# A shifted-window layer followed by a Fourier layer: one clamp moves to GpSimd, the second normalisation is written back to PSUM, and the transposes of x move between the halves of the second MLP layer

## The reference, cut to what matters

```
# layer 0, per window of 4x4 positions, 4 heads of 16 channels
qkv = xw @ qkv_w.T + qkv_b
qn = q / max(norm(q), 1e-12);  kn = k / max(norm(k), 1e-12)
attn = softmax(qn @ kn.T * scale + bias)
a = (attn @ v) @ proj_w.T + proj_b
x = x + layernorm(a) * g1 + b1
h = gelu(x @ fc1_w.T + fc1_b) @ fc2_w.T + fc2_b
x = x + layernorm(h) * g2 + b2
# layer 1: moving average over the rows plus a learned filter on the first 128
# Fourier modes of what is left; here it is a product with one matrix per channel
```

## Time and profile before

| what | value |
|---|---|
| median of 3 runs | 7964.86 us (7961.18 to 7968.6) |
| the profiled execution, its own time | 7957.41 us |
| its span on the core | 7955.6 us |
| PE busy | 6613.9 us (83%) |
| DVE busy | 6520.1 us (82%) |
| ACT busy | 5628.4 us (71%) |
| POOL busy | 5096.5 us (64%) |
| granted TensorE clock | 0.979 of full speed |

### The profile page before, as it was taken

One profiled execution on the slowest core, in us unless ns is written; L12 is line 12 of the kernel. 1 busy time (PEld: TensorE's weight loads), 2 busy tenths in 40 slices (PEclk: granted clock), 3 DMA queues, 4 the chain that ended last, 5 costly groups with the idle time before them and its releaser, 6 DMA issues.

```text
span 7955.6 us, 278088 instructions
## 1 busy us (share of the span) xinstructions
PE 6613.9 (83%) x105272; PEld 4133.5 (52%) x105272; DVE 6520.1 (82%) x8543; ACT 5628.4 (71%) x7004; POOL 5096.5 (64%) x4616
## 2 busy tenths in 40 slices
PE   8788888888888888888888888888888887787786
PEld 5544444444444444444444444444444444676675
DVE  1599999999999999999999999999999997222221
ACT  1488888888888888888888888888888888222221
POOL 0477777777777777777777777777777776000000
PEclk9899999999999999999999999999999999898898
DMA  2355555555555555555555555555555554999999
GB/s 98 112 148 147 146 145 145 146 147 146 146 146 146 146 146 146 145 145 146 147 147 146 147 146 146 147 146 146 144 145 147 147 146 124 331 332 354 342 332 338
DMA packets 1486082, 1370.67 MB, mean 172 GB/s; under 512 B 670097, under 2 KB 1080081, under 8 KB 1481875
## 3 DMA queue, kind: packets, MB, share of 16 engines
q1 hardware_dynamic: 1481412, 1235.63, 56.7%
q10 hardware_dynamic: 4608, 134.22, 4.0%
HBM read 412.97 MB, written 285.21 MB: 88 GB/s over the span
## 4 chain that ended last, share of the span: by engine, by line
DVE 49%; issue 29%; PE 14%; DMA 4%; DVEq 2%; ACT 0%; SPq 0%; POOL 0%; ACTq 0%; POOLq 0%
PE ps L632 10%; DVE arena L861 8%; DVE arena L879 8%; DVE ps L918 4%; DVE arena L884 4%; DVE arena L849 4%; DVE arena L933 4%; DVE arena L912 4%; DMA out<-arena 4%; DVE arena L899 4%; DVE arena L927 2%; DVE arena L873 2%; DVE arena L855 2%; PE ps L466 1%; DVEq L230 1%
## 5 line engine op out<-in xcount | busy, mean ns | idle before, releaser
L607 PE MATMUL ps<-mats,arena 128*64 128x512 f32 x4096 | 1083.3, 607 | 506.4 <-ACT mats L730 501.7
L595 PE MATMUL ps<-arena 64*128 64x512 f32 x4096 | 1017.5, 613 | 459.1 <-DVE arena L840 459.0
L997 POOL TENSOR_TENSOR arena<-arena 128x1024 f32<-128x1024 f32 x512 | 980.1, 1914 | 270.2 <-DVE arena L840 270.2
L730 ACT ACTIVATE mats<-ps,arena 128x1024 f32<-128x1024 f32 x1024 | 1133.1, 1107 | 0.0
L1004 POOL TENSOR_TENSOR arena<-arena 128x512 f32<-128x512 f32 x1024 | 1122.2, 1115 | 4.1 <-PE ps L551 4.1
L632 PE MATMUL ps<-rows,mats 128*128 128x256 f32 x4096 | 916.9, 388 | 234.6 <-ACT arena L751 159.4
L1036 POOL TENSOR_TENSOR arena<-arena 128x512 f32<-128x512 f32 x512 | 541.7, 1058 | 742.4 <-DVE arena L893 742.4
L963 DVE COPY arena<-ps 128x512 f32 x256 | 269.3, 1067 | 880.5 <-PE ps L632 564.0
L632 PEld LDWEIGHTS ps<-rows,mats 128*128 128x128 f32 x4096 | 796.9, 195 | 355.0 <-ACT arena L751 163.3
L595 PEld LDWEIGHTS ps<-arena 64*128 64x128 f32 x4096 | 373.5, 185 | 1129.7 <-issue 586.4
L1042 POOL TENSOR_TENSOR arena<-arena 128x512 f32<-128x512 f32 x512 | 566.8, 1107 | 544.7 <-DVE arena L906 544.7
(11 more groups left out here) (94 smaller groups left out, 15274.2 us busy)
## 6 DMA issues: line engine op xcount, KB each, us to landing
arena<-arena SPq DMA_DIRECT2D x1024, 256.0 KB, 2.7
rows<-arena SPq DMA_DIRECT2D x4096, 64.0 KB, 2.0
arena<-in_x SPq DMA_DIRECT2D x1024, 128.0 KB, 2.8
arena<-arena SPq DMA_DIRECT2D x1024, 128.0 KB, 2.3
y<-ystripe SPq DMA_DIRECT2D x512, 256.0 KB, 3.3
mats<-mix SPq DMA_DIRECT2D x512, 256.0 KB, 3.4
rows<-y SPq DMA_DIRECT2D x512, 256.0 KB, 4.1
out<-arena ACTq DMA_DIRECT2D x32, 4096.0 KB, 27.2
```

What stands on the lines that cost most here:

```text
L595: ins = mm(M[:, a, :], w1[a * C:a * C + C, kk * P:(kk + 1) * P], x1T[ring(g, 2)][a * C:a * C + C, :], start=True, stop=True, tile_position ...
L607: ins = mm(H2[a * C:a * C + C, :], w2[:, kk, :], hT[kk][:, a, :], start=(kk == 0), stop=(kk == 1), tile_position=(0, a * C))
L730: f(hT[kk], M, ACT.Gelu, bias=b1[:, kk:kk + 1]).then_inc(done, 1)
L997: tt(sq, q, q, ALU.mult).then_inc(squared, 1)
```

## The change

Three edits. `clamp` (a maximum with 1e-24 of 128 x 64 numbers) is taken from DVE and put on POOL, between `expand_v` and `add2`; `sum_squares` now waits until the clamp of the group before has read its input. `normed2` writes its result back into H2 instead of dn2 (the tile goes away), `gain2` reads H2, and `second_layer` waits for `gain2` (`yg_sb`) instead of `normed2` (`dn2_sb`). On PE, `turn_x` moves from ahead of `project` to between the two halves of `second_layer`.

```diff
-        sq1, sq1x, sq2, dn2, yg = (carve(512) for _ in range(5))
+        sq1, sq1x, sq2, yg = (carve(512) for _ in range(4))
...
                         if kk == 0:
                             need(pe, gelu0, g)
-                            need(pe, dn2_sb, before(g))
+                            need(pe, yg_sb, before(g))
...
                 scores(i4)
-                turn_x(i0)
                 project(i7)
                 second_layer(i9, 0, fc2a_ps)
+                turn_x(i0)
                 second_layer(i9, 1, fc2b_ps)
...
                 def sum_squares(g):
                     if there(g):
                         need(dve, squared, g)
+                        need(dve, clamped, before(g))
...
-                def clamp(g):
-                    if there(g):
-                        need(dve, summed, g)
-                        need(dve, logged, before(g, 2))
-                        ts(ssc[ring(g, 2)], ss, 1e-24, None, ALU.max).then_inc(clamped, 1)
...
-                        stt(dn2, H2, be2, r12[:, 1, :], ALU.add, ALU.mult).then_inc(dn2_sb, 1)
+                        stt(H2, H2, be2, r12[:, 1, :], ALU.add, ALU.mult).then_inc(dn2_sb, 1)
...
-                        ts(yg, dn2, g2, o12, ALU.mult, ALU.add).then_inc(yg_sb, 1)
+                        ts(yg, H2, g2, o12, ALU.mult, ALU.add).then_inc(yg_sb, 1)
...
                 sum_squares(i2)
-                clamp(i2)
                 bias(i4)
...
+                def clamp(g):
+                    if there(g):
+                        need(pool, summed, g)
+                        need(pool, logged, before(g, 2))
+                        settled(pool)
+                        pool.tensor_scalar(ssc[ring(g, 2)], ss, 1e-24, None, ALU.max).then_inc(clamped, 1)
...
                 expand_v(i5)
+                clamp(i2)
                 add2(i10)
```

## The result

The changed kernel takes 7743.22 us (median of 4 runs, 7742.71 to 7744.98) against 7963.02 us before (7959.75 to 7968.6): 0.9724 of the time, 95% interval 0.9707 to 0.9741. It is 220 us faster, where 348 were forecast; the measured time lies inside the stated range of 7480 to 7790 us.

What follows compares the result with a forecast made beforehand. DVE, 96% busy, bounded the 12.57 us step; then a loop through H2 would, at 6.08 + 3.74 + 1.66 + 0.39 = 11.87 us. Saving 0.70 x 502 = 351 us gives 7615 us, range 7480 to 7790.

Steps and rivals of the forecast that it cites:

- DVE was the bound and is not any more: Layer 0: DVE, 96% busy, bounds the old step; afterwards it needs 11.01 us and idles ahead of `normed1`.
- The clamp leaves DVE for almost nothing on POOL: Clamp: takes 1.19 us per step from DVE and costs POOL about 0.3 us, for which POOL has room.
- The rival that ended on the slower side: Clamp on POOL: above 1.83 us it exceeds the old step; at 2.5 us the kernel takes 8301 us; slower, chance 0.05.
- The new wait: PE's second layer waits for `gain2`, closing a one-step loop over PE, ACT and DVE that sets the step at 11.87 us.
- The size of the loop: Loop through H2: ACT 6.08, DVE 3.74, PE 1.66, hand-overs 0.39, together 11.87 us, with ends 11.63 and 12.35.
- The way from the transposes to `log_norms`: Part of the loop through H2, added up over ACT: `keep_x`, table load, `square2`, norms, exponentials; 0.31 us idle left out.
- The dearer loop: Rival at `normed2` and `gain2`: PSUM pause or POOL wait lengthens the loop to about 12.15 us, 7754 us; chance 0.20.
- By itself the transposes' move costs no instruction: PE: moving `turn_x` adds no instruction, starts `project` 0.58 us earlier, but puts 0.66 us of transposes in the loop.
- The fast form never runs at its speed here, so the edit gains: `gain2` on DVE: out of SBUF it waits for POOL, slot 0.97 us; out of PSUM 0.68 us, slot 0.60.

Runs made afterwards that it cites:

- two_logs: The changed kernel with `log_norm` on ACT done twice, once into a spare tile: 7745.71 us, ratio 0.9727 to the kernel before.
- turn_alone: The kernel before with only the transposes moved between the halves of the second layer, clamp and second normalisation as before: 7995.05 us, ratio 1.0039.

## Why the prediction was right, and where it was off

- **DVE was the bound and is not any more.** Right: 96% became 93%, with a mean of 0.45 us idle ahead of `normed1` in each step.
- **The clamp leaves DVE for almost nothing on POOL.** Right: it took 0.37 us where 0.3 was put, and doubling it changed nothing. Its wait of 0.93 us for the sums was not in the forecast. The rival that ended on the slower side, a clamp of over 1.83 us, did not occur.
- **The new wait closes a loop of one step.** Right, and shown: the chain of the changed kernel runs through it, taking 0.62 us out of it by the order of DVE's queue gained 262 us, and the edit in PSUM is free where the transposes are not behind its wait.
- **The size of the loop,** 11.87 us, was too small; it is 12.14. This is the step that was off: 0.27 x 502 = 135 us, about the 128 us missed. Term by term, forecast against the turn shown above: `gain2` with its hand-over 0.73 against 0.86, since 0.68 us was taken from a copy and a tensor_scalar out of PSUM takes 0.81; the first half of the second layer 1.00 against 1.08; from the transposes to `log_norms` 4.76 against 4.80; `normed1` and `add1` 1.69 against 1.74; `turn_prob` and `normed2` 1.37 against 1.38; `log_norms`, `root_norms` and the hand-over to `normed1` 2.32 against 2.24. That makes 12.10 us for this turn; the mean is 0.04 us higher, which was not followed further.
- **The way from the transposes to `log_norms`** was named wrongly, and its sum, 4.76 against 4.80 us, came out near by luck. It was added up over ACT; it runs over PE, and two_logs shows it: 0.25 us more on ACT is free. The row was there: ACT's 0.31 us of idle time ahead of `log_norms`, which the sum left out, said that PE's way ended later. ACT's own way is some 0.3 us shorter than forecast, in part because L692 starts 0.26 us behind L686 where it was 0.41 (a wait for POOL's `shift`, 16.6 us in 159 steps before, has gone), and because the hand-over from the transposes is 0.17 us where 0.23 was put. Two errors of about the same size cancel.
- **The dearer loop** (12.15 us, 7754 us) is what came out in size, but not by its mechanism: there is no pause between `normed2` and `gain2` (4053.66 follows 4052.98 by 0.68 us in the chain), and `gain2` is not blocked by POOL. So writing and reading one PSUM bank is not by itself what makes the pause before `add1`; what does was not tested.
- **"By itself the transposes' move costs no instruction"** was right and not enough. With the clamp on GpSimd it costs 120 us beside the edit in PSUM and gains 179 us without it, and alone it loses 33 us.
- **"The fast form never runs at its speed here, so the edit gains"** held only where the clamp stays on DVE. With the clamp off DVE and the transposes moved, `gain2` out of SBUF meets GpSimd at another moment and has a mean of 0.69 us, below the 0.81 us out of PSUM:

```profile
L934 DVE TENSOR_SCALAR arena<-arena 128x512 f32<-128x512 f32 x173 | 118.8, 687 | 6.4
```

By the Trainium skill (VectorE: DVE Perf Modes, section Why PSUM operands drop a tier) a float32 operand in PSUM loses the two-per-cycle mode. The two rows agree in direction: 0.81 us each time out of PSUM, and 0.69 us, blocks included, out of SBUF. In size no run shows it: the shortest `gain2` out of SBUF in this kernel took 0.545 us, where the prediction's estimate was 0.33. The difference of 0.12 us is also not what the edit costs here; its 294 us come from the loop.

## What to carry to other kernels

When the fullest engine is relieved in a software pipeline, the next bound need not be the next fullest engine: look for closed loops of waits that come round once per step, add up their durations and hand-overs from the trace, and follow each fork of the way. Ask of every edit what it puts behind which wait: releasing a buffer one instruction later was free until another edit placed the transposes behind that release. Try each edit alone and without each of the others, since their gains don't add up: here -333, -85 and +33 us alone, -220 us together, and -513 us for the best two.

## What the runs showed of the hardware that was not expected

- A tensor_scalar of 128 x 512 float32 with two per-partition operands takes 0.81 us out of PSUM; a copy of the same size takes 0.67 us.
- GpSimd does a clamp of 128 x 64 numbers in 0.37 us; with 32 numbers and two inputs it took 0.25 us.
- When DVE's copy (`regroup_x`) waits for GpSimd, it seems to go ahead of the next GpSimd instruction, whose record begins at its usual place but is longer: `divide` has 1.25 us in the changed kernel where it had 1.11, while `norm_q` ahead of it has its usual 1.06 us. The copy's record, from 4049.06, ends 0.31 us after `divide`'s record has begun:

```profile
4048.82 1.06 POOL L1028 TENSOR_TENSOR arena<-arena 128x512 f32<-128x512 f32 x1
4049.06 1.09 DVE L855 COPY arena<-arena 128x512 f32<-128x512 f32 x1
...
4049.84 1.24 POOL L1043 TENSOR_TENSOR arena<-arena 128x512 f32<-128x512 f32 x1
```

- In turn_alone the granted TensorE clock fell to 0.55 for one batch of products behind a pause of 1.57 us, where it was 1.00 in another step with a pause of 1.39 us. 17 of 159 batches were slow in this way, behind pauses of 1.37 to 1.59 us, and the waits of DVE behind them come to some 77 us, more than the 33 us that the move lost.
